# First-layer bias of the routed experts as a bf16 one-hot matmul, with one gelu for four tiles

## What is computed

```python
def _experts(ctx, idx, w1, b1, w2, b2):          # E = 8 experts, hidden width 64
    for e in range(E):
        h = _gelu(ctx @ w1[e] + b1[e])           # exact gelu; b1 is not zero
        o = h @ w2[e] + b2[e]
        out = out + jnp.where((idx == e)[:, None], o, 0)

for _ in range(2):                               # two iterations
    ctx = concat([integrated, v])                # v = 0 in the first
    shared_ctrl = _gelu(ctx @ shared_w1 + shared_b1) @ shared_w2 + shared_b2
    ctrl = _experts(repeat(ctx, 2), flat_idx, ...)   # top 2 of 8 experts per token
    ...                                          # gates, softplus, weighted sum, update
out = xf + integration_weight * (_gelu(integrated @ refine_w1 + refine_b1) @ refine_w2 + refine_b2)
```

## Time and profile before

| | us |
|---|---|
| median of 3 runs | 1163.74 (1163.22 to 1165.54) |
| profiled execution | 1175.17, its span 1173.4 |
| TensorE, VectorE, ScalarE, GpSimd busy | 886.9, 679.0, 565.5, 506.1 |
| routed part (from 643.6 to the end) | 529.8 of the span |
| gelus L1197 | 160, 44.5 busy |
| hidden matmuls L1608 | 480 records, 80.4 busy |

### The profile page before, as it was taken

One profiled execution on the slowest core, in us unless ns is written; L12 is line 12 of the kernel. 1 busy time (PEld: TensorE's weight loads), 2 busy tenths in 40 slices (PEclk: granted clock), 3 DMA queues, 4 the chain that ended last, 5 costly groups with the idle time before them and its releaser, 6 DMA issues. The chain is left out here.

```text
span 1173.4 us, 13996 instructions
## 1 busy us (share of the span) xinstructions
PE 886.9 (76%) x3906; PEld 607.2 (52%) x3906; DVE 679.0 (58%) x1536; ACT 565.5 (48%) x1036; POOL 506.1 (43%) x435
## 2 busy tenths in 40 slices
PE   2798899565878876888997671787676888888666
PEld 1466666443434443667676450565553655556344
DVE  5512221454475675764755950887964878697734
ACT  1733333434322123655655210877665767677621
POOL 3332200342344446240320757762775577454073
PEclk9989999776998996999999665966768989888678
DMA  9900000000000000000000012445555764633222
GB/s 356 400 1 1 1 0 0 1 0 0 1 1 0 0 1 0 1 1 1 0 0 6 22 37 72 130 149 174 179 183 166 232 195 141 191 118 115 59 67 79
DMA packets 71415, 90.33 MB, mean 77 GB/s; under 512 B 18685, under 2 KB 57597, under 8 KB 69373
## 3 DMA queue, kind: packets, MB, share of 16 engines
q1 hardware_dynamic: 60974, 64.02, 16.8%
q0 software_dynamic: 10240, 25.18, 6.8%
q10 hardware_dynamic: 144, 0.46, 0.2%
HBM read 43.49 MB, written 46.14 MB: 76 GB/s over the span
## 5 line engine op out<-in xcount | busy, mean ns | idle before, releaser
L544 POOL DMA_INDIRECT KEEP<-moved,small x128 | 134.4, 1050 | 148.5 <-issue 64.4
L534 POOL DMA_INDIRECT slots<-KEEP,small x128 | 134.8, 1053 | 49.6 <-issue 37.0
L1590 PE MATMUL PS<-TEMP,KEEP 65*128 x320 | 117.0, 508 | 22.0 <-ACT TEMP L1185 21.8
L1608 PE MATMUL PS<-KEEP,TEMP 128*64 128x128 f32 x480 | 80.4, 332 | 27.5 <-ACT KEEP L1212 23.0
L1185 ACT ACTIVATE TEMP<-PS 128x512 f32<-128x512 f32 (+2 forms) x92 | 51.4, 561 | 99.9 <-DVE TEMP L886 99.7
L1608 PEld LDWEIGHTS PS<-KEEP,TEMP 128*64 128x64 f32 x480 | 68.2, 170 | 50.8 <-ACT KEEP L1212 28.0
L886 DVE COPY TEMP<-PS 128x256 f32<-128x256 f32 (+1 forms) x92 | 42.8, 477 | 87.1 <-PE PS L1579 57.0
L1590 PEld LDWEIGHTS PS<-TEMP,KEEP 65*128 65x128 f32 x320 | 66.5, 223 | 49.7 <-issue 34.6
L480 POOL TENSOR_TENSOR KEEP<-KEEP 128x1024 f32<-128x1024 f32 x32 | 61.7, 1951 | 64.4 <-PE PS L1439 61.5
L1488 PE MATMUL PS<-TEMP_R 128*128 128x512 f32 x288 | 77.4, 421 | 11.8 <-POOL TEMP_R L507 8.2
L763 DVE TENSOR_TENSOR TEMP_R<-KEEP,TEMP_R 128x512 fp32r<-128x512 f32 x64 | 62.4, 1000 | 34.1 <-ACT KEEP L1145 33.6
(11 more groups left out here) (220 smaller groups left out, 2004.7 us busy)
## 6 DMA issues: line engine op xcount, KB each, us to landing
slots<-LX SPq DMA_DIRECT2D x14, 1024.0 KB, 25.0
moved<-LX SPq DMA_DIRECT2D x20, 512.0 KB, 3.0
TEMP<-slots SPq DMA_DIRECT2D x20, 512.0 KB, 4.4
TEMP<-experts SPq DMA_DIRECT2D x80, 64.5 KB
TEMP<-slots SPq DMA_DIRECT2D x20, 256.0 KB, 3.2
moved<-LX SPq DMA_DIRECT2D x20, 256.0 KB, 2.7
TEMP<-early SPq DMA_DIRECT2D x1, 2829.0 KB, 12.2
TEMP<-experts SPq DMA_DIRECT2D x80, 32.5 KB
```

The costliest lines, as they stand in the source:

```text
L534: pool.indirect_dma_start(dst, bass.IndirectOffsetOnAxis(ap=pos[:, h, 2 * m + k:2 * m + k + 1], axis=0), src, None).then_inc(SC[h], 16)
L544: pool.indirect_dma_start(G[:, n % 4, k, 0:w], None, src, bass.IndirectOffsetOnAxis(ap=pos[:, h, 2 * m + k:2 * m + k + 1], axis=0))\
L1590: last = pe.matmul(o, hT[0:EHID + 1, e % 3, P * j:P * (j + 1)], EW2[0:EHID + 1, bass.ds(at[j], n)], start=True, stop=True)
L1608: last = pe.matmul(PS[0:EHID, bank, part], W1[:, e % 4, j, 1 + EHID * a:1 + EHID * (a + 1)], xTs[:, x % 2, a, part], start=a == 0, stop=a ...
```

## The change

The bias is split on the chip into three bf16 parts (`split_b1`, on VectorE) whose sum is the fp32 value, one row for each part and expert, 24 rows in all. The sort writes, for each half, a one-hot of each slot tile's expert in three copies (`hotb`). In `g_hidden` of an E group one bf16 matmul of 24 rows, 64 output rows and 512 columns (four tiles, the one-hot column broadcast 128 times) starts the accumulation over all four tiles, and the fp32 matmuls add to it. The gelu then has no bias and covers 64x512 at once. W1 and the experts' rows lose column 0.

```diff
@@ -38,8 +38,10 @@
     ("mu", 1), ("murow", 128), ("shw", 1), ("fw1", 256), ("fb1", 2), ("fw2", 256), ("fb2row", 128), ("iwrow", 128),
+    ("eb1", EHID), ("which", 4),
 ]
-EXPERT_N = 1 + 2 * EHID
+EXPERT_N = 2 * EHID
+SPLIT = 3 * EXPERTS
@@ -70,7 +72,7 @@
 sc0 sc1 g_in0 g_in1 g_in2 g_in3 y_out0 y_out1
-xs0 xs1 xs2 xs3 wa0 wa1 wa2 wa3 w_second
+xs0 xs1 xs2 xs3 wa0 wa1 wa2 wa3 w_second b1_v
 p_t p_h p_q a_x a_g a_t a_l v_b v_ab v_c v_el v_up
@@ -172,7 +174,7 @@
         TEMP = sb("TEMP", [P, TEMP_N])
-        LX = sb("LX", [P, 6 * SEQ + P + 2 * TILES_H])
+        LX = sb("LX", [P, 6 * SEQ + P + 3 * TILES_H + EHID // 2])
@@ -274,7 +276,7 @@
         XS = tx(8, TILES, 2 * P)
-        W1 = tx(4, TILES, 1 + 2 * EHID)
+        W1 = tx(4, TILES, 2 * EHID)
         EW2 = tx(EXPERTS * 384)
@@ -283,7 +285,7 @@
         xnb = TEMP[:, 0:NSEQ * SEQ].rearrange("p (a j d) -> p a j d", a=NSEQ, j=TILES)
-        tr_ = cut(TEMP, 8192 + 16 * (1 + 2 * EHID) + EXPERTS * 384 + 16 * 257)
+        tr_ = cut(TEMP, 8192 + 16 * 2 * EHID + EXPERTS * 384 + 16 * 257)
         triB, onesB = tr_(64).bitcast(BF16), tr_(64).bitcast(BF16)
@@ -300,10 +302,15 @@
         te2 = LX[:, 6 * SEQ + P:6 * SEQ + P + 2 * TILES_H].rearrange("p (a b) -> p a b", a=2).bitcast(I32)
+        hotb = LX[:, 6 * SEQ + P + 2 * TILES_H:6 * SEQ + P + 3 * TILES_H].bitcast(BF16).rearrange("p (a b) -> p a b", a=2)
+        b1s = LX[:, 6 * SEQ + P + 3 * TILES_H:6 * SEQ + P + 3 * TILES_H + EHID // 2].bitcast(BF16)
+        bt = cut(LX, 0)
+        b_hi, b_mid, b_lo = [bt(EHID // 2).bitcast(BF16) for _ in range(3)]
+        b_rest, b_last, b_one, b_two = [bt(EHID) for _ in range(4)]
         ixf = so(NT, 2)
         swc, hosw, nhosw, asw = so(1), so(1), so(1), so(1)
-        rf = TEMP[:, 8192 + 16 * (1 + 2 * EHID):8192 + 16 * (1 + 2 * EHID) + 4 * SEQ].rearrange("p (a b) -> p a b", a=2)
-        ot = TEMP[:, 8192 + 16 * (1 + 2 * EHID) + EXPERTS * 384:8192 + 16 * (1 + 2 * EHID) + EXPERTS * 384 + 2 * SEQ]\
+        rf = TEMP[:, 8192 + 16 * 2 * EHID:8192 + 16 * 2 * EHID + 4 * SEQ].rearrange("p (a b) -> p a b", a=2)
+        ot = TEMP[:, 8192 + 16 * 2 * EHID + EXPERTS * 384:8192 + 16 * 2 * EHID + EXPERTS * 384 + 2 * SEQ]\
             .rearrange("p (a j d) -> p a j d", a=2, j=TILES)
@@ -385,7 +392,7 @@
                 for j, r in enumerate(experts_of(h, i)):
-                    n = 1 + it * EHID
+                    n = it * EHID
                     sp.dma_start(W1[:, e % 4, j, 0:n], experts[bass.ds(r, P), 0:n]).then_inc(WA[e % 4], 16)
@@ -789,6 +796,25 @@
+            def split_b1():
+
+                b, which = wl("eb1")[0:SPLIT], wl("which")[0:SPLIT]
+                dve.wait_ge(S["w_late"], 16)
+                dve.tensor_copy(b_hi[0:SPLIT], b).then_inc(S["b1_v"], 1)
+                dve.wait_ge(S["b1_v"], 1)
+                dve.tensor_tensor(b_rest[0:SPLIT], b, b_hi[0:SPLIT], ALU.subtract).then_inc(S["b1_v"], 1)
+                dve.wait_ge(S["b1_v"], 2)
+                dve.tensor_copy(b_mid[0:SPLIT], b_rest[0:SPLIT]).then_inc(S["b1_v"], 1)
+                dve.wait_ge(S["b1_v"], 3)
+                dve.tensor_tensor(b_last[0:SPLIT], b_rest[0:SPLIT], b_mid[0:SPLIT], ALU.subtract).then_inc(S["b1_v"], 1)
+                dve.wait_ge(S["b1_v"], 4)
+                dve.tensor_copy(b_lo[0:SPLIT], b_last[0:SPLIT])
+                dve.tensor_scalar(b_one[0:SPLIT], b_hi[0:SPLIT], which[:, 0:1], None, ALU.mult).then_inc(S["b1_v"], 1)
+                dve.wait_ge(S["b1_v"], 5)
+                dve.scalar_tensor_tensor(b_two[0:SPLIT], b_mid[0:SPLIT], which[:, 1:2], b_one[0:SPLIT], ALU.mult, ALU.add).then_inc(S["b1_v"], 1)
+                dve.wait_ge(S["b1_v"], 6)
+                dve.scalar_tensor_tensor(b1s[0:SPLIT], b_lo[0:SPLIT], which[:, 2:3], b_two[0:SPLIT], ALU.mult, ALU.add).then_inc(S["b1_v"], 1)
+
             def r_norm(t):
@@ -843,6 +869,7 @@
                 dve.wait_ge(S["so_v"], z + 9)
+                dve.tensor_scalar(hotb[0:SPLIT, h], tef[0:SPLIT], wl("which")[0:SPLIT, 3:4], None, ALU.is_equal)
                 dve.tensor_scalar(te2[:, h], tef, float(EXPERTS - 1), 384.0, ALU.min, ALU.mult)
@@ -862,6 +889,7 @@
                 r_norm(t)
+            split_b1()
             dve.tensor_copy(triB, wl("before"))
@@ -1193,9 +1221,7 @@
                         act.wait_ge(S["p_q"], UNIT_AT[EXP_G[e - 3] + 1])
-                    for j in range(TILES):
-                        last = act.activation(hT[0:EHID, e % 3, P * j:P * (j + 1)], PS[0:EHID, bank, P * j:P * (j + 1)],
-                                              ACT.Gelu, bias=W1[0:EHID, e % 4, j, 0:1])
+                    last = act.activation(hT[0:EHID, e % 3], PS[0:EHID, bank, :], ACT.Gelu)
                 else:
@@ -1602,11 +1628,17 @@
                     pe.wait_ge(WA[e % 4], 64 * (e // 4 + 1))
+                    if e == 0:
+                        pe.wait_ge(S["b1_v"], 7)
+                    if i == 0:
+                        pe.wait_ge(S["so_v"], SORT_N * h + 11)
+                    hot = hotb[0:SPLIT, h, TILES * i:TILES * (i + 1)].unsqueeze(2).to_broadcast([SPLIT, TILES, P])
+                    pe.matmul(PS[0:EHID, bank, :].rearrange("p (j d) -> p j d", j=TILES), b1s[0:SPLIT], hot, start=True, stop=False)
                     for j in range(TILES):
                         for a in range(it):
-                            last = pe.matmul(PS[0:EHID, bank, part], W1[:, e % 4, j, 1 + EHID * a:1 + EHID * (a + 1)],
-                                             xTs[:, x % 2, a, part], start=a == 0, stop=a == it - 1)
+                            last = pe.matmul(PS[0:EHID, bank, part], W1[:, e % 4, j, EHID * a:EHID * (a + 1)],
+                                             xTs[:, x % 2, a, part], start=False, stop=a == it - 1 and j == TILES - 1)
                 else:
@@ -1745,6 +1777,9 @@
     put("iwrow", everywhere(f["integration_weight"]))
+    put("eb1", np.concatenate([f["expert_b1"]] * 3))
+    put("which", np.concatenate([np.repeat(np.eye(3, dtype=np.float32), EXPERTS, 0),
+                                 np.tile(np.arange(EXPERTS, dtype=np.float32), 3)[:, None]], 1))
     return a
@@ -1752,9 +1787,8 @@
     f = {n[len("L1_ffn_"):]: v for n, v in i.items() if n.startswith("L1_ffn_")}
-    a[:, 0:EHID, 0] = f["expert_b1"]
-    a[:, :, 1:1 + EHID] = f["expert_w1"][:, :P]
-    a[:, :, 1 + EHID:1 + 2 * EHID] = f["expert_w1"][:, P:]
+    a[:, :, 0:EHID] = f["expert_w1"][:, :P]
+    a[:, :, EHID:2 * EHID] = f["expert_w1"][:, P:]
     return a.reshape(EXPERTS * P, EXPERT_N)
```

## The result

The median after is 1177.39 us (1175.09 to 1179.80, 4 runs) against 1163.48 (1159.85 to 1165.54, 4 runs) beside it: ratio 1.0097, 95% interval 1.0052 to 1.0143. That is slower, and above the top of the range. By the medians that is +13.9 us. Twelve more runs of the same kernel in a later group gave 1.0078 (1.0050 to 1.0105), some 9 us, and twelve on a chip where the kernel before takes 1251 us gave 1.0060 (1.0020 to 1.0100). Executions of one kernel fall into faster and slower ones, and each ratio and interval here uses only those within 1.5% of the kernel's fastest, while medians and ranges are over all of them.

A forecast was written before the change was run, and what follows sets the result against it. No engine was full: the routing chain, compute in the first and last expert phases, and GpSimd between them bound the kernel. Terms -3.0 + 2.5 + 5.0 + 0.1 = +4.6 us gave 1168.3, put at 1168.0 us, range 1160.5 to 1173.5.

The forecast's parts named there:

- phase one: First expert phase, last of the first 32 scatters to first gather: three shorter gelus and two one-hot matmuls on the path.
- the middle phases: Phases two and three, 811 to 1006 us: GpSimd's gathers and scatters cover compute, so the length stays the same.
- item 3: Bias split on VectorE between r_norm and the first logits: delays everything after it, +5.0 us, low end 2.0.
- Rival C: The split is nearly free because GpSimd's holds miss it: 2.0 us instead of 5.0, 1165.3 us; chance 16%.
- item 1: One gelu for four in 40 groups: 0.43 us less each, seven on the path, -3.0 us; ScalarE loses 17.2 us.
- item 2: Added one-hot matmul in 40 groups, 0.45 us at the low clock or 0.23 at the full: +2.5 us on the path.
- 2 x 0.45 in phase one: Two one-hot matmuls on the path of the first expert phase, each 0.45 us at the low clock.
- B: The clock eats the loss: three drops in the last phase vanish, -4.3 us, 1164.0 us; chance of this gain 9%.
- three drops added: Reverse of B: three clock drops come on top, 1172.6 us; chance 12% together with D.
- D: TensorE becomes the bound: all 20 outer one-hot matmuls on the path, +9.0, 1176.1 us; 12% together with drops added.
- A: ScalarE is the path in most groups: 15 to 20 outer gelus count, about -4 us, 1160 us; chance 13%.
- The last phase: From 1012.3 us to the last store at 1115.4: four gelus saved, four one-hot matmuls added, length within 2 us of before.

The follow-up runs named there:

- split_late: Kernel after with the bias split moved behind the second sort; 1168.75 us, ratio 1.0019 to the kernel before.
- no_onehot: Kernel after without the one-hot matmul, leaving out the experts' first-layer bias, single gelu kept; 1167.10 us, ratio 1.0010.
- rows128_b: Kernel after with the one-hot matmul over 128 rows, rows 24 to 127 zero, split in its old place; 1165.76 us, ratio 0.9978.
- late128_b: Kernel after with the split behind the second sort and the one-hot matmul over 128 rows; 1162.59 us, ratio 0.9918.
- four_gelus: Kernel after with four gelus of 64x128 without bias for the single one, one-hot matmul kept; 1173.10 us, ratio 1.0059.
- onehot_twice: Kernel after with each 24-row one-hot matmul issued twice, on a chip where before takes 1250.90 us; 1259.54 us, ratio 1.0041.
- after_again: Kernel after, unchanged, on a chip where the kernel before takes 1250.90 us; 1260.28 us, ratio 1.0060.
- late24z: Kernel after with the split behind the second sort and the zeroing memset, still 24 rows, slow chip; 1269.53 us, ratio 1.0109.
- late128: Kernel after with the split behind the second sort and the one-hot matmul over 128 rows, slow chip; 1252.91 us, ratio 0.9983.
- after_third: Kernel after, unchanged, run again beside a kernel before of 1166.59 us; 1175.26 us, ratio 1.0078.
- second_b: Kernel after with split behind the second sort, single gelu and one-hot matmul in the second iteration only; 1159.93 us, ratio 0.9961.
- second_c: Same kernel as second_b, run again beside a kernel before of 1165.49 us; 1162.33 us, ratio 0.9962.
- after: The changed kernel in its first runs and profile; 1177.39 us, ratio 1.0097.
- fourth group: Runs of kernel after with split late, varying one-hot rows (24, 64, 128) or gelus, beside a kernel before of 1264.93 us; ratios 0.9971 to 1.0112.

## Why the prediction was wrong

The forecast was 1168.0 us with a range up to 1173.5; measured were 1177.4, and by the later ratio some 1173. The stages give +4.7 for the split, +8.2 in phase one, -3.1 in the middle phases and -2.4 in the last, where the sum had +5.0, -0.4, nothing and -0.1. So phase one is the term that was wrong upwards; what was gained behind it, and not foreseen, hides part of that, and by the stages alone the time would have stayed in the range. What the first result has beyond the stages, 6.5 us, is open.

**The split (item 3) was right.** 5.0 us were forecast, by a walk through holds that each had a row; it was 4.7, by the three holds walked: subtract, cast, and the last cast with the tensor_scalar beside it. `split_late` took the 4.7 us ahead of the logits away. Rival C (2.0 us) fell. By the Trainium skill, "SBUF — State Buffer", section "SBUF: two separate sides", the second subtract passes the memset and a cast does not; the trace agrees, 0.21 us at 661.89 and 1.15 at 662.14.

**The gelu (item 1) was right in size, not in place.** 0.58 us instead of 1.00, ScalarE 20.4 us less (17.2 forecast). In phase one `no_onehot` got 2.7 us of it where three gelus were to give 1.3. The middle phases were costed at nothing and gave 1.3 and 1.8 us. Phase two has them without the one-hot matmul too (`no_onehot` 85.7) and not with four gelus (87.0), but `split_late`, with the single gelu, has 87.7. Phase three has them with both halves and 24 rows (86.8 to 87.7), hardly with 128 rows (`rows128_b` 88.4, `late128_b` 87.9), and not in `no_onehot` and `four_gelus` (88.8 each); no run tells why.

**The one-hot matmul (item 2) was the step that failed.** Its own length was a little short: the next matmul starts 0.56 us behind it at the lower clock and 0.33 at the full one, against 0.45 and 0.23, a tenth of a microsecond per group and not what made the loss. What failed is the sum that followed: "2 x 0.45 in phase one", each matmul costed by its own length with the clock of the groups left as it was, so that phase one came out at -0.4 and was measured at +8.2. Phase one of before had TensorE at 62 of 80 us, and I read the remainder as slack. But it was slack at a mean clock of 0.74. At the lower level a group's TensorE work in the kernel after is 0.56 + 1.90 + 0.90 + 3.56 = 6.92 us (one-hot, hidden, turn, control, each to the start of the next), as long as the group itself: nothing of the shorter gelu counts then. The control matmuls alone take 3.62 us there and 1.89 at the full clock. The expensive quantity was not the 0.45 us added, but the level at which all the others run.

**The rivals.** B had the mechanism, by its reverse: "three drops added". It was sized by single groups of the last phase and so gave 1172.6; it was a stretch of 51 to 61 us, and in phase one. D (TensorE becomes the bound, 1176.1) is what the timeline shows in that stretch, but its price came from twenty one-hot matmuls at 0.45 us and not from the whole group at the lower clock; that 1176.1 lies near the measured 1177.4 is luck, for it puts +9.0 on both outer phases together, where phase one alone lost 8.2 and the last lost nothing. Its test, `onehot_twice`, ran on the other kind of chip, with 7.4 us more in phase one than `after_again` and no more time in all. A (ScalarE is the path) is true where the clock is high and TensorE waits for it, `rows128_b` at 754.27 among others. That this is why the same kernel with 128 rows loses nothing, although it still pays for the split, fits its stages (phase one 1.3 us and phase two 1.6 under before), but no run shows it by itself.

That the low clock makes the loss is shown by `late24z` against `late128` (same instructions, 16.8 us in phase one) and `after_third` against `rows128_b` (8.0 us). That the long stretch needs both halves of the change at 24 rows is shown by `no_onehot` (20.5 us) and `four_gelus` (27.3), in one profile each. Why the clock answers to this matmul's rows, no run says.

The Trainium skill, "TensorE: Matmul & The Clock Gate", section "HAM oscillation — how this bites in real kernels", has the clock fall after idle gaps and stay up when they are closed. The traces do not bear this out here: in the kernel after TensorE ran without a gap from 741.55 to 804, and for 61.4 us of that at the lower level, while `rows128_b`, with gaps of 1.5 to 2.8 us ahead of most of its one-hot matmuls, had a mean clock of 0.80. Measurement decides.

**The last phase** was forecast unchanged, within 2 us. Means give -2.4, but the three profiles of before reach from 90.0 to 95.8, and the gain is all against the two high ones. `second_b` and `second_c` are 0.4% faster than before as a whole, with the change in the second iteration alone and phase one at 85.7 and 85.5, which speaks for a small gain behind phase one, at the limit of what the runs tell; how it divides over the phases is open.

## What to carry to other kernels

Where TensorE's clock moves between its levels within a stage, compute the engine's load of a group at the lower level too: if that alone fills the group, any small addition and any shorter wait elsewhere can leave the stage there, and the price is that of all its matmuls, not of the one added. Test a change by halves and together, because here one half gained 2.7 us in its phase, the other cost 3.7, and both together cost 7 to 10. Compare stages in profiles with the same clock: a stage that no edit touched took 15.4 or 19.4 us by it. A preparation on VectorE belongs behind a step that scatters or loads already cover, and its cost beside a busy GpSimd was here three holds of 1.1 to 1.3 us, which a walk through the rows gave well.

## What the runs showed of the hardware

**Zero rows paid here.** Going from 24 or 64 rows of contraction to 128, with zeros in the new ones, raised the granted clock of phase one from 0.61 and 0.64 (`after`, `after_third`) to 0.80 and 0.74 (`rows128_b`, `late128_b`), from 0.54 and 0.55 to 0.67 in the fourth group, and in the second only from 0.66 to 0.68.

**A matmul of few rows delays the next one.** At the lower clock the next matmul started 0.43 us behind the one of 128 rows (765.81 to 766.24 in `rows128_b`) and 0.56 behind the one of 24 or of 64; at the full clock 0.24 and 0.33. In `onehot_twice` the second one-hot matmul started 0.43 or 0.24 us behind the first, and the hidden matmul of 128 rows 0.56 or 0.31 behind the second, so the extra tenth comes where 128 rows follow fewer. The prediction took 0 for it. Whether it has to do with the clock is not shown.

**On some chips the whole core starts phase one late.** Where the kernel before took 1251 and 1265 us, the first three groups of expert weight loads were issued over 7.4 to 13.5 us each. SyncE's timeline of `late24z`, its groups of four loads:

```profile
719.59 13.45 SPq L396 DMA_DIRECT2D TEMP<-experts  x4
...
739.36 12.71 SPq L396 DMA_DIRECT2D TEMP<-experts  x4
...
758.39 8.16 SPq L396 DMA_DIRECT2D TEMP<-experts  x4
...
767.73 1.89 SPq L396 DMA_DIRECT2D TEMP<-experts  x4
```

and of the kernel after on the chip of its first profile:

```profile
726.50 1.89 SPq L396 DMA_DIRECT2D TEMP<-experts  x4
```

The other engines stood still in the same time, by the timelines of `late24z` (TensorE, VectorE's copy of the controls, ScalarE's first expert gelu and its copy of turned tokens):

```profile
767.68 0.63 PE L1637 MATMUL PS<-LX 24*64 24x512 bf16 x1 [27.39 <-ACT KEEP L1239]
...
766.20 0.42 DVE L915 COPY TEMP<-PS 128x256 f32<-128x256 f32 x1 [28.48 <-remote]
...
761.94 0.59 ACT L1225 ACTIVATE KEEP<-PS 64x512 f32<-64x512 f32 x1 [23.80 <-remote]
...
766.94 0.68 ACT L1239 ACTIVATE KEEP<-PS,WL 128x512 f32<-128x512 f32 x1
```

TensorE waited for ScalarE: L1239 ended at 767.62, 0.06 us ahead. ScalarE's gelu at 761.94 waits by its program only for its hidden matmul, which had ended at 729.24, and the engine had been free since 738.15; "remote" means that the profile names no instruction that released it. So the slow loads are not shown to be the cause: SyncE, ScalarE and VectorE were all late together, and no row tells what held them. All eight profiles from the two chips show slow loads and a standstill of TensorE of 21 to 31 us; of the kernel before there are only times. Phase two is longer there too (99 to 108 us against 85 to 88), so ratios from such a chip weigh a change differently, and a stage is only compared between kernels on one chip.
